# Cross attention in a decoder layer: GpSimd selects two heads of four, copies and score products in another order

## The reference, cut to what matters

```python
scores = jnp.einsum('bthd,bghd->bhtg', Q, K) / np.sqrt(DH)
scores = jnp.where(vision_mask[:, None, None, :], scores, -jnp.inf)
topv, topi = jax.lax.top_k(scores, K_TOP)          # 32 of 2048
probs = jax.nn.softmax(topv, axis=-1)
attn = jnp.zeros_like(scores).at[bi, hi, ti, topi].set(probs)
attn_mean = attn.mean(axis=1)                      # over the 4 heads
c_t = jnp.einsum('btg,bgd->btd', attn_mean, V)
```

## Time and profile before

| what | value |
|---|---|
| median of three timed runs | 4725.45 us (4723.23 to 4727.43) |
| span of the profiled execution | 4717.9 us, 63502 instructions |
| the profiled execution's own time | not given apart from its span; the timed runs lie 5.3 to 9.5 us above the span |
| TensorE busy (products) | 4022.0 us, 85% |
| VectorE busy | 2652.5 us, 56% |
| ScalarE busy | 1462.9 us, 31% |
| GpSimd busy | 1356.0 us, 29% |
| the stage of the cross attention | about 1057 to 2297 us of the span |

### The profile page before, as it was taken

The page is one execution under the profiler, slowest core; times in us unless marked ns, Lnnn a source line. Parts: engine busy times, 40 slices in busy tenths (PEclk is TensorE's granted clock), DMA queues, the critical chain, the costliest instruction groups (busy, mean ns, idle before and its releaser), DMA issues. The chain is left out here.

```text
span 4717.9 us, 63502 instructions
## 1 busy us (share of the span) xinstructions
PE 4022.0 (85%) x20972; PEld 3288.8 (70%) x20972; DVE 2652.5 (56%) x8700; ACT 1462.9 (31%) x2339; POOL 1356.0 (29%) x1161
## 2 busy tenths in 40 slices
PE   6846799966866888888799697959999999999998
PEld 4722677745766777778688575747778787878786
DVE  8745355519999999999455454224434346222222
ACT  2354233336545666566200101212111112111111
POOL 0000111102112121131266032024777665323332
PEclk8668899987988999989899898979999999999999
DMA  1143322261010110100244333341222123000000
GB/s 59 37 151 113 102 87 87 71 212 42 20 38 28 29 47 15 48 28 10 90 141 140 105 119 132 112 161 56 71 74 69 56 83 92 25 19 25 23 25 18
DMA packets 248594, 336.94 MB, mean 71 GB/s; under 512 B 67524, under 2 KB 125764, under 8 KB 245958
## 3 DMA queue, kind: packets, MB, share of 16 engines
q1 hardware_dynamic: 151976, 177.79, 12.6%
q10 hardware_dynamic: 93744, 146.84, 9.2%
q0 software_dynamic: 2560, 8.39, 0.5%
HBM read 220.70 MB, written 112.25 MB: 71 GB/s over the span
## 5 line engine op out<-in xcount | busy, mean ns | idle before, releaser
L3085 DVE CAST m_act_hl<-m_g 128x512 fp32r<-128x512 f32 x256 | 138.6, 541 | 849.4 <-ACT m_g L2953 849.1
L1632 PE MATMUL xa_ps_t<-xa_diag,xa_s_buf 128*128 128x128 f32 x4096 | 502.6, 283 | 129.6 <-DVE xa_s_buf L1840 78.8
L1632 PEld LDWEIGHTS xa_ps_t<-xa_diag,xa_s_buf 128*128 128x128 f32 x4096 | 485.2, 197 | 160.7 <-DVE xa_s_buf L1840 97.4
L1788 DVE MAX8 xa_cand<-xa_s_buf 128x8 f32<-128x64 f32 x4096 | 539.4, 219 | 36.4 <-issue 13.5
L2779 POOL TENSOR_TENSOR m_act_hl<-m_g,m_act_hl 128x512 fp32r<-128x512 f32 x256 | 354.5, 1385 | 678.1 <-DVE m_act_hl L3085 678.1
L2953 ACT ACTIVATE m_g<-m_ps_h,m_b 128x512 f32<-128x512 f32 x256 | 176.2, 688 | 1116.7 <-PE m_ps_h L82 1111.6
L80 PE MATMUL m_ps_h<-m_hT,m_w 128*128 128x512 f32 x1024 | 417.2, 407 | 19.8 <-issue 17.7
L1560 POOL TENSOR_TENSOR xa_aT<-xa_a,xa_aT 128x512 fp32r<-128x512 f32 x128 | 160.8, 1277 | 869.0 <-ACT xa_a L1712 869.0
L82 PE MATMUL m_ps_h<-m_hT,m_w 128*128 128x512 f32 x1024 | 409.7, 400 | 0.0
L81 PE MATMUL m_ps_h<-m_hT,m_w 128*128 128x512 f32 x1024 | 409.6, 400 | 0.0
L80 PE MATMUL m_ps_o<-m_w,m_act_hl 128*128 128x512 f32 x1024 | 406.7, 397 | 0.7 <-POOL m_act_hl L2779 0.7
(11 more groups left out here) (373 smaller groups left out, 8142.4 us busy)
## 6 DMA issues: line engine op xcount, KB each, us to landing
at_xk<-in_x_dram SPq DMA_DIRECT2D x128, 128.0 KB, 2.7
spectrum<-df_yo ACTq DMA_DIRECT2D x32, 512.0 KB, 2.8
id_raw<-spectrum SPq DMA_DIRECT2D x32, 512.0 KB, 5.7
m_xt<-x ACTq DMA_DIRECT2D x64, 256.0 KB, 3.6
ky_raw<-in_ctx_dram SPq DMA_DIRECT2D x16, 768.0 KB, 6.2
xa_ks<-kt SPq DMA_DIRECT2D x48, 256.0 KB
xa_raw<-in_ctx_dram SPq DMA_DIRECT2D x32, 384.0 KB, 3.7
w<-bf_out_t SPq DMA_DIRECT2D x32, 256.0 KB, 2.5
```

The lines of the kernel that those rows point to most:

```text
L1632: last = pe.matmul(ps_t[:, c // 4, c % 4, :], s_buf[:, t % 2, h, k0:k0 + P], diag[:, h, :], start=(h == 0 and c % 4 == 0), stop=(h == HEAD ...
L1788: dve.max(out=ranks[h][:, :, g], in_=s_buf[:, t % 2, h, :].rearrange("p (n g e) -> p g n e", g=SEGS, e=4)[:, g, :, :])
```

## The change

Five things change in `stage_cross`. GpSimd gets a `select` of its own, two instructions with a drain between: compare with the threshold, in place, then multiply by `prob`. It takes heads 2 and 3, in the first tile of a batch only head 3 (`first_pool_head`); VectorE keeps the others. GpSimd does it ahead of `lo(t, 0)` and, at a batch's start, ahead of `context_lo` 0 to 3. A new semaphore, `s_psel`, counts those selections; TensorE's turns of these heads, ScalarE's exponentials 0 and 1 (whose place in `prob` GpSimd read in the tile before) and VectorE's `settle` (which may use `prob`) wait for it. On TensorE, `scores(t+1,1)` moves from this iteration's start into the second half of the last iteration's turns, `scores(t+1,3)` ahead of the first half, `scores(t+2,0)` into its middle. On ScalarE the copies move likewise: the copy of head 1 to the end of the iteration before, that of head 2 ahead of `diagonals`, that of head 3 ahead of exponential 3.

```diff
+        s_psel = sem("selected_by_gpsimd")
+        def first_pool_head(t):
+            return 3 if t % TPB == 0 else 2
...
@@ gpsimd
+                def select(t, h):
+                    row = s_buf[:, t % 2, h, :]
+                    pool.wait_ge(s_exp, HEADS * t + h + 1)
+                    pool.tensor_scalar(row, row, top[:, t % 2, h, TOPK - 1:TOPK], None, ALU.is_ge)
+                    pool.drain()
+                    pool.tensor_tensor(row, row, prob[:, h % 2, :], ALU.mult).then_inc(s_psel, 1)
...
                     if t >= 1:
                         lo(t - 1, 2)
                         lo(t - 1, 3)
+                    for h in range(first_pool_head(t), HEADS):
+                        select(t, h)
                     if new:
                         for g in range(4):
                             context_lo(b, g)
@@ tensor
                     if half == 0:
-                        pe.wait_ge(s_sel, HEADS * t + h + 1)
+                        if h < first_pool_head(t):
+                            pe.wait_ge(s_sel, dve_heads(t, h))
+                        else:
+                            pe.wait_ge(s_psel, pool_before[t] + h - first_pool_head(t) + 1)
...
                 scores(1, 0)
+                scores(1, 1)
                 for t in range(TILES):
                     sum_rows(t)
-                    if t + 1 < TILES:
-                        scores(t + 1, 1)
                     sum_flags(t)
                     if t + 1 < TILES:
                         scores(t + 1, 2)
                     if t >= 1:
                         mix(t - 1)
+                    if t + 1 < TILES:
+                        scores(t + 1, 3)
                     turn(t, 0, 0)
                     turn(t, 0, 1)
-                    if t + 1 < TILES:
-                        scores(t + 1, 3)
+                    if t + 2 < TILES:
+                        scores(t + 2, 0)
                     turn(t, 0, 2)
                     turn(t, 0, 3)
+                    turn(t, 1, 0)
+                    turn(t, 1, 1)
                     if t + 2 < TILES:
-                        scores(t + 2, 0)
-                    for h in range(HEADS):
-                        turn(t, 1, h)
+                        scores(t + 2, 1)
+                    turn(t, 1, 2)
+                    turn(t, 1, 3)
@@ scalar
                     if t >= 1 or h >= 2:
-                        act.wait_ge(s_sel, HEADS * t + h - 1)
+                        if h >= 2:
+                            act.wait_ge(s_sel, dve_heads(t, h - 2))
+                        else:
+                            act.wait_ge(s_sel, dve_heads(t - 1, h + 2))
+                            act.wait_ge(s_psel, pool_before[t - 1] + h + 3 - first_pool_head(t - 1))
...
                     row_sums(t)
-                    if t + 1 < TILES:
-                        copy(t + 1, 1)
...
                     exponentials(t, 1)
-                    diagonals(t)
                     if t + 1 < TILES:
                         copy(t + 1, 2)
+                    diagonals(t)
                     exponentials(t, 2)
-                    exponentials(t, 3)
...
                     if t + 1 < TILES:
                         copy(t + 1, 3)
+                    exponentials(t, 3)
...
                         copy(t + 2, 0)
                     if new:
                         context_hi(b, 6)
+                    if t + 2 < TILES:
+                        copy(t + 2, 1)
@@ vector
                 def settle(t):
+                    if t >= 1:
+                        dve.wait_ge(s_psel, pool_before[t])
...
                     if more:
                         scan(t + 1, 2, 0, SEGS)
-                    if t >= 0:
+                    if t >= 0 and first_pool_head(t) == 3:
                         select(t, 2)
-                        select(t, 3)
```

More of the change, by code:

```diff
@@ L1479, in stage_cross, with dve_heads @@
         flags = cand_b[:, :, :].rearrange("p h n -> p (h n)").bitcast(BF16).rearrange("p (h a x) -> p h a x", h=HEADS, a=2)
+        def first_pool_head(t):
+            return 3 if t % TPB == 0 else 2
+        pool_before = [0]
+        for t in range(TILES):
+            pool_before.append(pool_before[-1] + HEADS - first_pool_head(t))
+        def dve_heads(t, h):
+            done = sum(first_pool_head(i) for i in range(t))
+            return done + min(h + 1, first_pool_head(t))
         with nc.Block() as block:
@@ L1729, in _ @@
                 copy(1, 0)
+                copy(1, 1)
                 act.wait_ge(s_const, 3)
```

## The result

The changed kernel takes 5138.76 us (median of 4 runs, 5138.17 to 5140.95) against 4724.57 for the kernel before (median of 4): ratio 1.0877, 95% interval 1.0862 to 1.0892, so 414 us slower. The direction and the mechanism were as forecast; the size was not (forecast 212 slower, range up to 350 slower).

A forecast was written before the change was run, and what follows sets the result against it. The prediction took a second loop through GpSimd's selections to bound the kernel: 28 ordinary tiles at 6.7 us more (42.4 each) and four batch-start tiles at 6 more add 212 to 4725, giving 4937 us, range 4830 to 5075.

The forecast's parts named there:

- DVE's 141 us: 60 selections of 2.343 us taken off VectorE, forecast to return as waiting for the flags, some 8 us in each tile.
- The second loop: From sum_rows through flags, exponentials, selection and turns to the next tile's sum_rows: 39.4 us forecast without clock loss.
- Front of the loop: From sum_rows to the end of the exponential of head 2: +12.8 us forecast, +15.2 before the change.
- the inserted score product: `scores(t+2,1)` within the second half of the turns on TensorE, forecast to add 1.4 us to a tile.
- The compare: GpSimd's threshold compare over 128x2048 for each head it selects: 2.0 us, worked out from affine select and memset rows.
- the bound that I had set from above: GpSimd's compare was to stay below its two-tensor product, 4.55 us for 2048 columns.
- TensorE's clock: Gaps while TensorE waits for GpSimd's selections slow its later turns: 3.0 us per ordinary tile, bounds 0 and 4.6.
- Batch-start tiles: Four tiles with context work, `context_lo` delayed behind GpSimd's selection of head 3: about +6 us each, bounds 3 and 10.
- The sum: Whole kernel: 28 x 6.7 + 4 x 6 = 212 us added to 4725.
- Rival 2: Slow compare on GpSimd: 5032 us in all at 3.6 us each, far end 5136 at 4.55 us; chance 22%.
- No meeting of DVE's selections with POOL's in ordinary tiles: VectorE's two selections end at about +12 from sum_rows, GpSimd's begin at +12.9; a meeting would cost 1.6 to 2.2 us.

## Why the prediction was right or wrong

- *That DVE's 141 us come back as idle time*: right. DVE waits 13.1 us in the shown tile, though mostly for a score copy (10.57) and not, as forecast, for the flags (2.53).
- *The second loop and its order*: right, in each piece. Front of the loop +12.7 (forecast +12.8); a product 4.51 (4.55); the gap between compare and product 0.14 (0.15); second half behind the turn, and the inserted score product, as worked out.
- *The compare*: wrong, and it is the step that failed, a term of the sum mis-sized: 5.44 us instead of 2.0, 6.9 us per ordinary tile. It lies even above the bound that I had set from above, the product's 4.55, "since it reads one tensor fewer": on GpSimd one tensor with a scalar takes longer (5.36 to 5.45 us alone) than two tensors (4.49). The Trainium skill, "GPSIMD Engine Reference", section "Engine selection", calls one-input operations roughly line-rate; the copy's 1.89 us agrees, the 5.4 of compare, multiply and subtract with a scalar doesn't, and the measurement decides.
- *TensorE's clock, 3.0 us*: about right. From the turn of head 3 to sum_rows 15.8 us in the shown tile, at a granted clock of 0.77, after waits of 6.79 and 6.50 us for GpSimd; at the full clock I had worked out 13.1: 2.7 more.
- *Batch-start tiles, +6*: +10.7, +9.1, +7.4 and +8.1, 8.8 in the mean, 3.4 of it the compare. So 5.4 for the rest, near the 6.
- *The sum, with the measured compare*: 28 x 13.6 + 4 x 9.4 = 418, measured 414. Rival 2 at its far end (5136) named the right cause, and I gave it 22% in all and kept its far end out of the range. That it also came within 3 us of the time is luck: its compare of 4.55 was 1.8 us per tile too short for two heads, and its clock loss of 4.6 was 1.9 too long. The fault was to take one row as near because its name said compare, and then to let it narrow the range.
- *No meeting of DVE's selections with POOL's in ordinary tiles*: right for the selections; but other instructions met, without cost here (4.46 us for four columns of `nmax`).

## What to carry to other kernels

Busy time says what an engine could take over; where the work stands in the loop that closes a tile says whether it may. Work for a slower engine is looked for where its result is needed late: here the same engine with half the columns, started some 8 us later in the tile and needed only by the second half of the turns, turned 414 us of loss into 36 of gain. An operation that no row shows is measured by itself before it is bounded by a row that only resembles it.

## What the runs showed of the hardware

On GpSimd, f32, 128 x 2048: copy and affine select 1.89 us, product of two tensors 4.49, compare and multiply with a scalar (per row or constant) and subtract with one per row 5.36 to 5.45, subtract and max in one instruction 7.16. VectorE's `tensor_scalar` on 128 x 4, 0.16 us in the median before, took 4.46 behind a GpSimd product, which fits the Trainium skill, "SBUF — State Buffer", section "Who interferes with whom", that the shared ports are held for a whole instruction; a compare on GpSimd likewise took 6.67, 1.2 more, when it started 1.36 us before the end of a selection on VectorE. The views of that `tensor_scalar`, before and after (ns least/median/most):

```profile
L1812 DVE TENSOR_SCALAR xa_nmax<-xa_top x32: 154/161/1783, 1083.9 to 2259.0; 128x4 f32<-128x4 f32 x32
...
L1844 DVE TENSOR_SCALAR xa_nmax<-xa_top x32: 164/4461/4464, 1086.9 to 2639.2; 128x4 f32<-128x4 f32 x32
```
